# Attention chain by batch in a fused pooled-attention and mixture-of-experts layer on one Trainium2 core: an order of steps rewritten

## What is computed

```python
def attn(x, Wq, bq, Wqa, bqa, Wk, bk, Wka, bka, Wt, bt):   # b = 2, s = 2048, 16 heads
    mixed_q, mixed_k = x @ Wq + bq, x @ Wk + bk
    q_w = softmax((mixed_q @ Wqa + bqa) * scale, axis=1)      # over all tokens of a batch
    pooled_q = einsum('bsh,bshd->bhd', q_w, heads(mixed_q)).reshape(b, 1, dm)
    mixed_qk = mixed_k * pooled_q
    k_w = softmax((mixed_qk @ Wka + bka) * scale, axis=1)
    pooled_k = einsum('bsh,bshd->bhd', k_w, heads(mixed_qk))
    return (pooled_k[:, None] * heads(mixed_q)).reshape(b, s, dm) @ Wt + bt + mixed_q

x = x + attn(layernorm(x), ...)
x = x + experts(layernorm(x), ...)     # RMS norm, router, 2 of 8 experts per token, one shared expert
```

## Time and profile before

| | us |
|---|---|
| median of 3 runs | 794.44 (794.03 to 796.34) |
| profiled execution | 793.84 |
| its span | 792.1 |
| TensorE busy | 736.6 (93%) |
| VectorE busy | 567.1 (72%) |
| ScalarE busy | 439.4 (55%) |
| GpSimd busy | 185.7 (23%) |

### The profile page before, as it was taken

One profiled execution on the slowest core, in us unless ns is written; L12 is line 12 of the kernel. 1 busy time (PEld: TensorE's weight loads), 2 busy tenths in 40 slices (PEclk: granted clock), 3 DMA queues, 4 the chain that ended last, 5 costly groups with the idle time before them and its releaser, 6 DMA issues. The chain is left out here.

```text
span 792.1 us, 11674 instructions
## 1 busy us (share of the span) xinstructions
PE 736.6 (93%) x4254; PEld 609.3 (77%) x4254; DVE 567.1 (72%) x1179; ACT 439.4 (55%) x739; POOL 185.7 (23%) x163
## 2 busy tenths in 40 slices
PE   3587999679998999999999999999999999999997
PEld 3344566457786888898888989888888989898876
DVE  6734566388686377767967878777867878786994
ACT  3531133545436465848558565846749485847342
POOL 2200111000000312443532543543432443220000
PEclk9978999899999999999999999999999999999999
DMA  9300022103000153544645575455744675353870
GB/s 328 137 1 1 8 73 80 54 0 114 1 1 0 35 186 116 194 160 152 222 156 186 180 255 162 160 163 168 242 155 156 188 245 160 114 195 112 272 235 29
DMA packets 45801, 106.93 MB, mean 135 GB/s; under 512 B 9293, under 2 KB 33744, under 8 KB 38064
## 3 DMA queue, kind: packets, MB, share of 16 engines
q1 hardware_dynamic: 38928, 88.49, 33.9%
q0 software_dynamic: 6816, 17.71, 6.9%
HBM read 89.39 MB, written 17.69 MB: 135 GB/s over the span
## 5 line engine op out<-in xcount | busy, mean ns | idle before, releaser
L884 ACT ACTIVATE hid<-psU,b 128x512 f32<-128x512 f32 (+2 forms) x280 | 154.8, 581 | 212.1 <-issue 147.9
L657 PE MATMUL psD<-w,hhi 128*128 128x512 f32 x824 | 218.3, 405 | 13.0 <-DVE x_sb L1181 7.4
L1159 DVE TENSOR_TENSOR hlo<-hid,hhi 128x512 fp32r<-128x512 f32 x206 | 139.7, 691 | 72.9 <-ACT hhi L887 70.9
L657 PEld LDWEIGHTS psD<-w,hhi 128*128 128x128 f32 x824 | 148.9, 191 | 48.4 <-DVE x_sb L1181 8.9
L631 PE MATMUL psU<-xhl,w 128*128 128x512 f32 (+2 forms) x560 | 146.4, 343 | 3.7 <-ACT xhl L824 2.1
L637 PE MATMUL psU<-xhl,w 128*128 128x512 f32 (+2 forms) x560 | 146.7, 343 | 0.0
L633 PE MATMUL psU<-xhl,w 128*128 128x512 f32 (+2 forms) x560 | 146.2, 342 | 0.0
L397 POOL DMA_INDIRECT xin<-token_in,src x71 | 79.6, 1121 | 272.2 <-PE psT L607 131.6
L1187 DVE TENSOR_TENSOR w<-raw,w 128x1024 fp32r<-128x1024 f32 x112 | 132.7, 1218 | 1.9 <-ACT w L780 1.9
L405 POOL DMA_INDIRECT token_out<-fold,dst x71 | 87.9, 1237 | 141.5 <-DVE fold L1181 133.8
L663 PEld LDWEIGHTS psD<-w,hlo 128*128 128x128 f32 x824 | 110.9, 189 | 9.1
(11 more groups left out here) (194 smaller groups left out, 560.3 us busy)
## 6 DMA issues: line engine op xcount, KB each, us to landing
raw<-in_wpack SPq DMA_DIRECT2D x58, 1024.0 KB, 5.5
xT<-token_out SPq DMA_DIRECT2D x32, 256.0 KB, 4.8
x_sb<-in_x SPq DMA_DIRECT2D x8, 512.0 KB, 9.4
token_in<-z_sb SPq DMA_DIRECT2D x8, 512.0 KB, 2.9
out<-x_sb SPq DMA_DIRECT2D x16, 256.0 KB, 5.4
b<-in_b2pack SPq DMA_DIRECT2D x29, 128.0 KB, 5.3
att<-in_attn SPq DMA_DIRECT2D x1, 1379.0 KB, 11.5
xin<-token_in,src POOLq DMA_INDIRECT x71, 2.9
```

Of the source, the lines that this page charges most:

```text
L657: mm(acc, hhi[:, part], wpair[slot][:, :, c * D:(c + 1) * D], start=(c == 0), stop=False)
L884: last = nc.scalar.activation(hid[:, n % 4, i * rows:(i + 1) * rows], acc, ACT.Relu, bias=b1[:, u % 2, m:m + 1])
L1159: V.tensor_tensor(hlo[:, part], hid[:, n % 4, :], hhi[:, part].bitcast(F32), ALU.subtract).then_inc(hlo_ready, 1)
```

## The change

- Every semaphore of the attention chain exists once for each batch, and steps are named by (b, r). Batch 0's two rounds come first in the queues; batch 1's first round lies around the end of batch 0's, and its second between batch 0's projections.
- The first statistics are taken by groups of eight tiles (`GRP`), the second by eight tiles too, the last group split into two of four (`ZGRP`).
- The constants come in two transfers: 384 columns behind x chunk 0, and the rest (the unit matrix `eye`, the head mask `hm`, the tables) behind x chunk 7, with a semaphore `table_loaded`. `nw` comes behind x chunk 7 too. `fold_query` is not changed: it waits for `att_loaded` at 32.
- A projection starts with one bias matmul of 512 columns over both tiles, in place of one of 256 at the end of each tile. Banks are 0 and 2 for the first eight pairs, then q % 4.
- The low parts of the shared expert's matrices are made in halves (`first_lo`), later in VectorE's order.
- The up steps 0 and 1 of group 0 are set apart between the last turned pairs, 2 and 3 behind them.

```diff
+GRP = [(0, 8), (8, 16), (16, 24), (24, 32)]
+ZGRP = [(0, 8), (8, 16), (16, 24), (24, 28), (28, 32)]
...
             load_x(0)
-            load_x(1)
-            sp.dma_start(cst[:, :], consts).then_inc(cst_loaded, 16)
-            load_x(2)
-            load_x(3)
+            sp.dma_start(cst[:, 0:C_EYE], consts[:, 0:C_EYE]).then_inc(cst_loaded, 16)
+            for c in range(1, 4):
+                load_x(c)
             sp.dma_start(att[:, :], attn).then_inc(att_loaded, 16)
-            sp.dma_start(nw[:, :], norm).then_inc(att_loaded, 16)
             for c in range(4, NC):
                 load_x(c)
+            sp.dma_start(nw[:, :], norm).then_inc(att_loaded, 16)
+            sp.dma_start(cst[:, C_EYE:C_ALL], consts[:, C_EYE:C_ALL]).then_inc(table_loaded, 16)
...
-            proj_bank = [(0, 2)[q % 2] if q < NT // 4 else (1, 3, 0, 2)[q % 4] for q in range(NT // 2)]
+            proj_bank = [2 * (q % 2) if q < NT // 4 else q % 4 for q in range(NT // 2)]
...
+                pair = psU[:, proj_bank[q], :].rearrange("p (t n) -> p t n", t=2)
+                mm(pair, one2[:, :], cpair[:, b:b + 1, :].to_broadcast([2, 2, D]), start=True, stop=False)
                 for tt in range(2):
                     t = 2 * q + tt
-                    dst = psU[:, proj_bank[q], tt * D:(tt + 1) * D]
                     for k in range(KD):
-                        mm(dst, xT[:, t // 4, k, t % 4 * P:(t % 4 + 1) * P], mt[:, b, k, :], start=(k == 0), stop=False)
-                    last = mm(dst, one2[:, :], cpair[:, b, :], start=False, stop=True)
+                        last = mm(pair[:, tt, :], xT[:, t // 4, k, t % 4 * P:(t % 4 + 1) * P], mt[:, b, k, :],
+                                  start=False, stop=(tt == 1 and k == KD - 1))
```

TensorE's new order (the lines added; the loop bodies of before fall away):

```diff
             fold_query()
             for q in range(4, 8):
                 turn_rows(q)
+            score(0, 0)
+            turn_max(0, 0)
             turn_rows(8)
+            spread_max(0, 0)
             turn_rows(9)
             turn_rows(10)
+            turn_probs(0, 0)
             turn_rows(11)
+            pool_rows(0, 0)
+            turn_pooled(0, 0)
+            project_pooled(0, 0)
             turn_rows(12)
             turn_rows(13)
+            fold_key(0)
             turn_rows(14)
+            score(0, 1)
             turn_rows(15)
+            turn_max(0, 1)
+            spread_max(0, 1)
+            score(1, 0)
+            turn_probs(0, 1)
+            turn_max(1, 0)
+            pool_rows(0, 1)
+            spread_max(1, 0)
+            turn_pooled(0, 1)
+            turn_probs(1, 0)
+            project_pooled(0, 1)
+            pool_rows(1, 0)
+            mix(0)
+            turn_pooled(1, 0)
+            project(0)
+            project_pooled(1, 0)
+            project(1)
+            fold_key(1)
+            project(2)
+            score(1, 1)
+            project(3)
+            turn_max(1, 1)
+            project(4)
+            spread_max(1, 1)
+            project(5)
+            turn_z(0)
+            turn_probs(1, 1)
+            turn_z(1)
+            project(6)
+            pool_rows(1, 1)
+            turn_z(2)
+            turn_pooled(1, 1)
+            project_pooled(1, 1)
+            project(7)
+            mix(1)
+            turn_z(3)
+            project(8)
...
+            project(11)
+            router(0)
+            project(12)
+            turn_z(8)
+            turn_z(9)
+            project(13)
+            turn_z(10)
+            turn_z(11)
+            project(14)
+            project(15)
             pe.wait_ge(w_lo[0], 1)
+            pe.wait_ge(x1_ready, NT // 2 - 3)
+            up(0, 0, (0,))
+            turn_z(12)
+            pe.wait_ge(x1_ready, NT // 2 - 2)
+            up(0, 0, (1,))
+            turn_z(13)
             pe.wait_ge(x1_ready, NT // 2)
+            up(0, 0, (2, 3))
+            turn_z(14)
+            turn_z(15)
             router(1)
```

VectorE's new order:

```diff
+            stats_of(0)
+            first_moments(0)
+            stats_of(2)
+            offsets(0)
+            normalise_even(0, 8)
+            first_moments(1)
+            folded_query()
+            stats_of(4)
+            offsets(1)
+            normalise_even(8, 16)
+            first_moments(2)
+            helpers()
+            row_max(0, 0)
+            offsets(2)
+            normalise_even(16, 20)
+            head_max(0, 0)
+            normalise_even(20, 24)
+            softmax_bias(0, 0)
+            stats_of(6)
+            first_moments(3)
+            reciprocal_sum(0, 0)
+            offsets(3)
+            normalise_even(24, 28)
+            add_groups(0, 0)
+            normalise_even(28, 32)
+            dve.wait_ge(table_loaded, 16)
             pooled_query(0)
...
+            first_lo(0, 0)
             pooled_query(1)
+            add_rows(0)
             folded_key(1)
+            add_rows(1)
+            add_rows(2)
+            row_max(1, 1)
+            head_max(1, 1)
+            second_moments(0)
+            add_rows(4)
+            softmax_bias(1, 1)
+            z_rows_even(0)
...
+            second_moments(2)
+            add_rows(12)
+            z_rows_even(2)
+            second_moments(3)
             turned_lo(0)
+            add_rows(14)
+            z_rows_even(3)
+            second_moments(4)
+            z_rows_even(4)
```

More of the change, by code:

```diff
@@ L848, in _, with rows_outs @@
[L848 to L861 removed]
+            def rows_outs(first, end):
+                for q in range(first, end):
+                    rows_out(q)
@@ new lines, in z_outs @@
+            def z_outs(first, end):
+                for q in range(first, end):
+                    z_out(q)
+            normalise_odd(0)
+            rows_outs(0, 4)
+            normalise_odd(1)
+            rows_outs(4, 8)
+            normalise_odd(2)
+            rows_out(8)
+            exponentials(0, 0)
+            rows_out(9)
+            probs_out(0, 0)
+            rows_outs(10, 12)
+            pooled_out(0, 0)
+            normalise_odd(3)
+            rows_outs(12, 16)
+            exponentials(0, 1)
@@ L862, in _ @@
+            logits_out(0)
+            z_rows_odd(2)
+            turned_hi(0)
+            z_outs(8, 12)
+            z_rows_odd(3)
+            z_outs(12, 14)
+            z_rows_odd(4)
+            z_outs(14, 16)
             logits_out(1)
@@ L983, in softmax_bias, with folded_query @@
-            def softmax_bias(i):
-                b = i % B
-                dve.wait_ge(max_ps, i + 1)
-                dve.wait_ge(fold_sb, 1 if i < B else 2 + b)
+            def folded_query():
+                dve.wait_ge(fold_ps, 1)
+                V.tensor_copy(aq[:].rearrange("p k h -> p (k h)"), psD[:, 0, C_FOLD:C_FOLD + KD * 32])
+                for b in range(B):
+                    last = V.tensor_tensor(small[:, b, 0:1], psD[:, 0, C_SB:C_SB + 1], att[:, A_BQA:A_BQA + 1], ALU.add)
+                last.then_inc(aq_ready, 1)
@@ new lines, in helpers, with row_max @@
+            def helpers():
+                link(V.tensor_reduce(own, ident.rearrange("p (g h) -> p h g", g=4), X, ALU.add))
+                V.tensor_copy(sel.rearrange("p (g h) -> p g h", g=4),
+                              own.rearrange("p (o h) -> p o h", o=1).to_broadcast([P, 4, 32]))
+                for n in range(KD):
+                    V.tensor_scalar(bqrep[:, n, :], ones[:, 0:32], att[:, A_BQ + n:A_BQ + n + 1], None, ALU.mult)
+                V.tensor_copy(one2[:], ones[0:2, :])
+            def row_max(b, r):
+                dve.wait_ge(score_ps[b], r + 1)
+                V.tensor_reduce(small[:, b, 1:2], psU[:, b, :], X, ALU.max).then_inc(rowmax_ready[b], 1)
```

441 lines of the change are left out of this document (178 added, 263 removed).

## The result

The changed kernel takes 783.21 us (median; 781.03 to 784.95), beside 795.07 us (794.03 to 796.34) for the kernel before on the same chip: a ratio of 0.9842, interval 0.9823 to 0.9861. That is 11.9 us by the medians and 12.6 by the ratio, and the forecast was 8.1. Its time lies inside the range (782.0 to 791.2), at the lower end.

A forecast was written before the change was run, and what follows sets the result against it. TensorE's expert part bounds the span and is unchanged, so only its start moves: batch 0's mix ends at 69.35, not 77.5 (8.15 earlier), the projection stage gives nothing, 794.44-8.1 = 786.3 us; range 782.0 to 791.2.

The forecast's parts named there:

- The start up to S: Until batch 0's first scores end: `fold_query` waits for late `nw`, so 33.0 against 31.34, 1.7 us later.
- Rival 3: At the start: `nw` doesn't hold anything, first scores end 4.7 earlier; gain 12.8, 781.6 us; chance 0.07.
- S to T: Batch 0's first to second scores' end: 24.75 before, 16.4 at full clock, by -4.1 pooling, -1.6 split, +1.1 turns.
- T to M: Batch 0's second scores' end to its mix's end: 21.4 before, 16.3 at full clock; fold and batch 1's scores -1.8.
- The clock: Low TensorE clock from batch 0's first scores to its mix: cost 7.3 before, half taken, 3.65; ends 0 and 7.3.
- M to the expert part: Batch 0's mix end to expert part, the projection stage: 80.3 before and 80.3 forecast, so no gain.
- term (a): Projections: the merged bias matmul saves 0.2 in each of 16, -3.2 us; bounds nothing or -5.0.
- (d): Projection stage: new waits of TensorE, 1.4 at `turn_z(0)`, 2.2 at `turn_z(8)`, short steps, bias row, copies, router; +7.4 us.
- fewer moment instructions: Projection stage: on VectorE beside TensorE's projections, claimed to be worth nothing by themselves.
- Rival 4: At the start: `nw` (128 pieces, issue 1.4 us) lands last, near 27.7; slower, 797.4 us; chance 0.05.
- rival 1: Projection stage gives back 3 to 5: merged bias saves nothing, or `turn_z(8)`'s wait drops the clock; 790.4; chance 0.17.

The follow-up runs named there:

- b_nw_late: Kernel before with only the norm weight's transfer issued behind x chunk 7: 800.09 us, ratio 1.0054 to the kernel before.
- b_max_first: Kernel before with batch 0's first maximum, exponentials and pooling set without the turns between them: 796.35 us, ratio 1.0005 to the kernel before.
- b_max_split: Kernel before with batch 0's maximum first and the split of the shared expert's first matrix moved later: 794.54 us, ratio 0.9995 to the kernel before.
- b_chain: Kernel before with batch 0's whole first round, fold included, ordered as in the changed kernel; batch 1's first scores still ahead: 797.27 us, ratio 1.0031.
- a_batch1_ahead: Changed kernel with batch 1's last turn and first scores ahead of batch 0's second scores: 787.67 us, ratio 0.9914 to the kernel before.
- a_nw_early: Changed kernel with the norm weight's transfer issued right behind the attention weights, ahead of x chunks 4 to 7: 776.85 us, ratio 0.9774 to the kernel before.
- a_bias_twice: Changed kernel with the old projection form, two bias matmuls of 256 columns: 787.52 us, ratio 0.9896 to the kernel before.
- b_bias_once: Kernel before with only the new projection form, one bias matmul of 512 columns first: 791.44 us, ratio 0.9956 to the kernel before.
- a_moments_twice: Changed kernel with each group of eight tiles taken in two sets of moments of four: 786.65 us, ratio 0.9910 to the kernel before.
- a_best: Changed kernel with `nw` early, `folded_query` later, `z_rows_even(2)` ahead of `add_rows(12)`, `turn_probs(1, 1)` and a projection ahead of `turn_z(0)`: 773.37 us, ratio 0.9717.

## Why the prediction came out as it did

**The stage and the mechanism: right.** The expert part starts 11.7 earlier and does the same work; the loss at the start, the gain between S and M, and a projection stage that gives little were each forecast, and the marks show each.

**The start up to S: right.** Forecast 1.7 later, measured 1.4. Its turns of pairs 4 to 7 took 3.94, as priced (0.97 each). One reading needs care: the earlier trace rows gives a clock of 1.00 for 0 to 27.7, and the profile of before gives 1.00 for 27.7 to 31.3 too, and yet the turns take 1.94 for eight, where they take 1.04 at 110.26 in the kernel after, and the first scores take 3.64 for 1.92. So at the start the low level shows in the durations and not in the clock column. `nw` landed at 21.2 (20.3), behind x chunk 7 (21.0); VectorE waited 6.69 (7). b_nw_late shows the same cause in the kernel before. The Trainium skill, DMA: Bandwidth & Descriptors, section Queues, rings and completion order, has a semaphore's increment land only after every earlier write of that DMA engine; by that rule `nw` could not pass x7, and the trace agrees: 21.2 against 21.0. Rival 3, that `nw` holds nothing, falls. Its price was right: with the wait gone S is 4.3 earlier, where it said 4.7.

**S to T: the sum right, its parts not.** Forecast 16.4 and half the clock's price there, about 2; measured 18.3. Two errors cancel, and that is luck. The work was priced 1.4 too long. Batch 0's pooling was to start 6.6 after S and started 5.5 after it: the 6.6 was read from T to the second pooling as a stretch in which nearly nothing stands between the chain's steps, but batch 1's first pooling stands in it (TensorE's timeline of the kernel before):

```profile
57.37 1.93 PE L509 MATMUL psD<-z_sb,xin 128*32 128x256 f32 x32 [0.19 <-ACT xin L790]
```

The low clock was priced too low: the granted clock is 0.57 from 43 to 51, where batch 0's second scores took 3.29 for 1.92 and the key's fold 1.91 for 0.97; with three turns and the fold's short matmuls it comes to 3.3, not 2. The prediction also wrote the stretch as terms that each bring something: 4.1 from the pooling, 1.6 from the split. In the kernel before, alone or together, they bring nothing (b_max_first, b_max_split, b_chain). The order that the prediction walked has batch 1's scores off the chain too, but it gave that no term. a_batch1_ahead does: about 5 us.

**T to M: the work term mis-sized.** Forecast 16.3 at the full clock, measured 16.8 with a clock of 0.90. In a_nw_early, where the clock is 1.00 throughout, the same stretch is 15.1, so the work is 1.1 to 1.2 shorter than the term. The clock's share was right here: 1.6 (0.63 from 60 to 64.6; the second pooling took 3.29 for 1.93, the pooled projection 1.22 for 0.96), against half of 3.3. The term named the fold and batch 1's scores; it left out the wait of 1.69 ahead of the mix, which is gone in the kernel after (the mix starts at 64.86, right behind the pooling). That this wait is the 1.1 was not tried by itself.

**The clock.** 3.65 was taken for S to M. By the durations above it cost 3.3 and 1.6, so 4.9, inside the ends of 0 and 7.3. M came 1.5 early because the work was priced 2.5 too long.

**M to the expert part: 2.0 too long, by term (a).** The bias matmul was priced at 3.2 with an upper bound of 5.0; the rows give 6.4. The hold was right (0.42, as the prediction wanted it to be), but the bound was drawn from the bias matmul alone, and the data matmuls behind it also got shorter. Against the 3.2 that this is more stands a low clock that the sum hadn't there, about 1.7: 1.38 in one projection (3.37 for 1.99), the rest in the second mix behind it (granted clock 0.72 from 97 to 103). **The new waits (d) came as forecast:** `turn_z(0)` 1.44 (1.4), `turn_z(8)` 2.32 (2.2), bias row (1) 0.83 (1.0), pooled 0.27 and 0.38 (0.4 and 0.6), router 1.22 (1.3); with the two copies, 0.5, that don't show they are 0.9 less than the 7.4. -3.2, +1.7 and -0.9 make -2.4; the 0.4 to the -2.0 lies in shorter rows. In the end time a_bias_twice and b_bias_once show 4.3 and 3.5 of the bias term; in the second the clock took a part of it back.

**One sentence was wrong:** that fewer moment instructions are worth nothing by themselves. a_moments_twice prices them at 3.4 to 5.4 in the end time, some 2 of it waits. The sum did not fail by it, since the waits of (d) were worked out with VectorE's orders in groups of eight; but a reader who took the sentence alone would leave 2 us or more.

**Rival 4's argument fell.** It took the 1.4 us of `nw`'s issue for a sign of a costly shape. The same transfer's issue took 0.43 in a_nw_early and 2.14 in the kernel after. Of rival 1, the two things that it named didn't happen in the kernel after: the bias matmul saved more, and the projection behind `turn_z(8)` took 1.99, the length at the full clock. But its mechanism is there: behind the same step, with waits of 2.32 and 2.40, the clock did fall in a_bias_twice (0.66 from 128 to 133) and in a_moments_twice (0.59).

**What stays open:** how much of the gain of a_nw_early is the wait and how much the clock that followed; and VectorE's waits for x in the kernel after (7.2 us in two, of them 4.3 for the first chunk, where before there was one, of 4.8), which are there in a_best too (6.7). That they come from the other order of the loads was not tried.

## What to carry to other kernels

A step of an in-order queue that waits is priced by what is queued behind it: put a tiny load that shares a semaphore with a large one right behind that one, or move the step that waits down the queue; either brought some 6 us here. Moving one step of a dependent chain up gave nothing here while the next step of the chain stands behind other work on its own engine; walk all queues up to the end of the chain before you believe a term, and write down which terms need each other. When you take a row for what a chain costs undisturbed, look at every line inside it for another batch's work. Size the work and the clock apart: the same stretch in another run at a clock of 1.00 shows the work alone. Where a new order puts a consumer right behind its producer, look for what the producer's queue still does in between.

## What the runs showed of the hardware that was not expected

The cost of issuing a transfer on SP is not that of the transfer. SP's timeline of the kernel after:

```profile
0.73 0.44 SPq L302 DMA_DIRECT2D x_sb<-in_x  x1
...
4.28 8.75 SPq L302 DMA_DIRECT2D x_sb<-in_x  x4
13.07 2.14 SPq L312 DMA_DIRECT2D nw<-in_norm  x1
15.26 0.43 SPq L313 DMA_DIRECT2D cst<-in_consts  x1
```

One x chunk takes 0.44 to issue at the start and four take 8.75 once the earlier ones are under way, and the 1 KB of `nw` took 0.43, 1.43 or 2.14 by its place. The 873 KB of constants issued right behind `nw` took 0.43 again. The runs show the times, not the reason.

A two-row bias matmul between two groups of four 128x256 data matmuls costs more than its hold of 0.31. Four data matmuls between two bias matmuls take 1.06 from start to start, eight take 1.93, and four that follow turned rows take 0.96 (93.57 to 94.53 in the kernel before). So it is some 0.1 for each group that stands behind a bias matmul, rather than a longer time of every data matmul. The ends of matmuls are modelled, so the starts are what this rests on.

The clock that one stretch gets differs between kernels that do the same in it. T to M had 0.90 in the kernel after, 1.00 in a_nw_early with the same work, and 0.73 in a_batch1_ahead, where batch 1's scores stand ahead of T and 20 matmuls fewer are left (16.8, 15.1 and 18.8 us). The length of the wait just ahead doesn't tell it either. Behind `turn_z(8)` a wait of 2.32 was followed by the high level in the kernel after and by the low one in a_bias_twice, and in a_best the projection that ran low in the kernel after is low as well (3.01 and 3.37, for 1.99), though the wait of 1.4 ahead of `turn_z(0)` is gone there and none over 0.4 is left in the 8 us before it. The Trainium skill, TensorE: Matmul & The Clock Gate, section HAM oscillation — how this bites in real kernels, describes waits for a transfer after each of which the matmuls start again at the slower clock. The trace agrees only in part: the low level at the start of the expert part does stand behind a wait (1.61), but in S to T of the kernel after TensorE is never idle for more than 0.8 at a time and falls to the low level all the same (1.00 from 32.7 to 43, then 0.57). What made it fall there no run shows.
